# The output written by POOL's indirect DMAs instead of SP's plain ones, in a three-stage macaron block on one core

## What is computed

```
def _L0_ffn_ref(x, gate_w, gate_b, w1, b1, w2, b2, w3, b3):
    logits = einsum('bsd,de->bse', x, gate_w) + gate_b
    probs = softmax(logits, axis=1)
    vals, idx = top_k(probs, 2)
    h = relu(einsum('bsd,edo->ebso', x, w1) + b1)
    h = relu(einsum('ebso,eop->ebsp', h, w2) + b2)
    y = relu(einsum('ebso,eop->ebsp', h, w3) + b3)
    onehot = one_hot(idx, E)
    w_tok = einsum('bske,bsk->bse', onehot, vals)
    ind = onehot.max(axis=2)
    v = einsum('ebso,bse->eo', y, w_tok)
    return einsum('bse,eo->bso', ind, v)

x = x + 0.5 * _L0_ffn_ref(_layernorm(x), ...)
x = x + _L0_attn_ref(_layernorm(x), ...)
x = x + 0.5 * _L0_ffn_ref(_layernorm(x), ...)
return x
```

## Time and profile before

| | |
|---|---|
| median of 3 runs | 1159.49 us (1155.8 to 1160.2) |
| the profiled execution | 1155.8 us, of which the span of the trace is 1154.0 us |
| busy PE / DVE / POOL / ACT | 1063.4 / 886.0 / 703.5 / 670.9 us |
| output, line L404 | 8 transfers of 256 KB by SP, landing 2.5 us after issue |

### The profile page before, as it was taken

One profiled execution on the slowest core, in us unless ns is written; L12 is line 12 of the kernel. 1 busy time (PEld: TensorE's weight loads), 2 busy tenths in 40 slices (PEclk: granted clock), 3 DMA queues, 4 the chain that ended last, 5 costly groups with the idle time before them and its releaser, 6 DMA issues.

```text
span 1154.0 us, 16851 instructions
## 1 busy us (share of the span) xinstructions
PE 1063.4 (92%) x5671; PEld 609.8 (53%) x5671; DVE 886.0 (77%) x1333; ACT 670.9 (58%) x899; POOL 703.5 (61%) x367
## 2 busy tenths in 40 slices
PE   4599999659999999999999999999999976899996
PEld 1376666335645655645655655654654523666663
DVE  9989999786766866866866866866764576999996
ACT  3388888435654654654654654654654643788882
POOL 3465555527785785785685685686685861555552
PEclk8799999879999999999999999999999988899999
DMA  5165473000101001001001001001001012576672
GB/s 151 41 136 120 97 121 73 19 1 3 39 20 38 20 21 38 20 21 38 21 20 39 20 21 38 20 20 38 20 20 39 21 38 64 87 118 101 108 110 73
DMA packets 43850, 59.25 MB, mean 51 GB/s; under 512 B 9829, under 2 KB 23174, under 8 KB 43782
## 3 DMA queue, kind: packets, MB, share of 16 engines
q1 hardware_dynamic: 43782, 58.37, 24.2%
HBM read 55.20 MB, written 2.62 MB: 50 GB/s over the span
## 4 chain that ended last, share of the span: by engine, by line
PE 60%; issue 17%; POOL 16%; DVE 6%; ACT 1%; POOLq 0%; DMA 0%; SPq 0%
PE ring L737 19%; POOL R L464 13%; PE ring L690 5%; PE ring L708 5%; PE ring L710 5%; PE ring L712 5%; PE ring L714 5%; PE ring L747 4%; PE ring L723 3%; DVE xn L1054 2%; PE ring L672 2%; POOL sum_picksT L425 1%; PE ring L674 1%; PE ring L673 1%; PE ring L647 1%
## 5 line engine op out<-in xcount | busy, mean ns | idle before, releaser
L1238 DVE TENSOR_REDUCE mx<-ring 128x2 f32<-128x1024 f32 x256 | 298.6, 1225 | 88.1 <-PE ring L690 88.1
L425 POOL TENSOR_TENSOR sum_picksT<-sum_picksT,P_wb 128x1024 f32<-128x1024 f32 x128 | 323.9, 2531 | 18.6 <-POOL sum_picksT L425 0.4
L924 ACT ACTIVATE P_wb<-ring 128x1024 f32<-128x1024 f32 x256 | 262.3, 1028 | 64.8 <-PE ring L714 40.2
L464 POOL TENSOR_TENSOR R<-t,R 128x512 fp32r<-128x512 f32 x128 | 171.1, 1337 | 160.7 <-ACT R L836 160.6
L425 POOL TENSOR_TENSOR sum_picksT<-P_wb 128x1024 f32<-128x1024 f32 x64 | 153.8, 2403 | 172.7 <-ACT P_wb L924 172.7
L737 PE MATMUL ring<-P_wb,t 128*64 128x512 f32 x1024 | 226.8, 595 | 0.0
L511 PE MATMUL ring<-R,whi 128*128 128x512 f32 (+1 forms) x384 | 170.0, 443 | 18.5 <-DVE R L1033 9.6
L513 PE MATMUL ring<-R,wlo 128*128 128x512 f32 (+1 forms) x384 | 153.1, 399 | 0.0
L512 PE MATMUL ring<-R,whi 128*128 128x512 f32 (+1 forms) x384 | 152.8, 398 | 0.0
L936 ACT COPY OZ<-ring 128x512 f32<-128x512 f32 x64 | 37.0, 587 | 199.1 <-PE ring L737 156.5
L737 PEld LDWEIGHTS ring<-P_wb,t 128*64 128x64 f32 x1024 | 70.6, 137 | 132.8 <-issue 128.4
(11 more groups left out here) (136 smaller groups left out, 1350.5 us busy)
## 6 DMA issues: line engine op xcount, KB each, us to landing
P_wb<-wd SPq DMA_DIRECT2D x14, 2048.0 KB, 15.5
rzb_indp<-rzd SPq DMA_DIRECT2D x64, 256.0 KB, 3.9
P_wb<-wd SPq DMA_DIRECT2D x8, 512.0 KB, 10.4
xs<-in_L_attn_x SPq DMA_DIRECT2D x8, 256.0 KB, 3.7
zrc<-SZ SPq DMA_DIRECT2D x128, 2.0 KB, 1.7
out<-xs SPq DMA_DIRECT2D x8, 256.0 KB, 2.5
sum_picksT<-in_L_ffn_w SPq DMA_DIRECT2D x2, 512.0 KB, 5.5
MR<-mT SPq DMA_DIRECT2D x64, 4.0 KB
```

The costliest lines, as they stand in the source:

```text
L425: pool.tensor_tensor(US[:, g % 2, c, :, :], first, PU[:, TPB * c + t, :, :], ALU.add).then_inc(s_ua, 1)
L464: pool.tensor_tensor(h2l[:, e % 2, :], t2[:, e % 2, :], h2h[:, e % 2, :].bitcast(F32), ALU.subtract).then_inc(s["h2_ready"], 1)
L924: act.activation(PU[:, u, :, :], ring[slot(("scores", g, u))][:, :, :], ACT.Exp, scale=SCALE).then_inc(s_exp, 1)
L1238: dve.tensor_reduce(mx[:, :, u], ring[slot(("max", g, u))][:, :, :], AX.X, ALU.max).then_inc(s_max, 1)
```

## The change

The output is no longer sent by SP. A new tile `rows` ([128, 32] of uint32) is filled by POOL at the very start of its program with `rows[p, t] = 128 t + p`, the number of the output row that partition p of token tile t belongs to. At the end of POOL's program, behind `experts(1)`, POOL waits for the same semaphore `x_updated` batch by batch, and for every token tile issues an indirect DMA: it takes the 128 rows of 512 bytes of `xs[:, t, :]` and writes each to the row of the output (seen as 4096 rows of 128 numbers) that `rows[:, t]` names. These are 32 transfers of 64 KB where there were 8 of 256 KB. POOL then waits for all 32 (`s_out` at 512). The bytes and their places are the same.

```
         xs = sb("xs", [P, NT, D])
+        rows = sb("out_rows", [P, NT], mybir.dt.uint32)
...
+        s_rowids = sem("out_row_numbers")
...
             weights_out(1)
-            for b in range(B):
-                sp.wait_ge(F[1]["x_updated"], b + 1)
-                sp.dma_start(out[b].rearrange("(j p) d -> p j d", p=P), xs[:, TPB * b:TPB * (b + 1), :]).then_inc(s_out, 16)
-            sp.wait_ge(s_out, 16 * B)
...
         def _(pool):
+            pool.iota(rows[:, :], pattern=[[P, NT]], base=0, channel_multiplier=1).then_inc(s_rowids, 1)
             pool.memset(ident[:, :], 0.0).then_inc(s_id0, 1)
...
             experts(1)
+
+            pool.wait_ge(s_rowids, 1)
+            table = out.rearrange("b s d -> (b s) d")
+            for b in range(B):
+                pool.wait_ge(F[1]["x_updated"], b + 1)
+                for j in range(TPB):
+                    t = TPB * b + j
+                    pool.indirect_dma_start(table, bass.IndirectOffsetOnAxis(ap=rows[:, t:t + 1], axis=0), xs[:, t, :], None
+                                            ).then_inc(s_out, 16)
+            pool.wait_ge(s_out, 16 * NT)
```

## The result

| | before | changed |
|---|---|---|
| median | 1158.03 us (4 runs, 1155.8 to 1160.2) | 1192.88 us (4 runs, 1192.35 to 1196.28) |
| ratio | | 1.0307, 95% interval 1.0277 to 1.0338 |
| profiled execution, its span | 1155.8, 1154.0 us | 1196.28, 1194.5 us |
| end of DVE's first addition to the end of the span ("the ending") | 10.0 us | 45.9 us |

The account below looks back on a forecast made before the run. PE was busy 92%, but the end was bound by DVE's last addition plus one landing. Ending 32 x 1.27 + 2.5 + 0.5 = 43.6 us against 10.0, +33.6 on 1159.49: 1193.1 us, range 1168 to 1230 us.

Follow-up runs that it names:

- one-by-one kernel: The changed kernel with POOL waiting for each indirect transfer's landing before it issues the next; spacing 2.50 us, ending 83.9 us.

## What to carry to other kernels

Count the issues that an engine must make after the last result exists, multiply by the spacing of issues back to back, and compare with the pace at which the producer hands out tiles: up to that pace they are free, above it the whole queue of issues, counted from the first tile, is the length of the ending. An indirect transfer costs its issuer nearly the same for 64 and for 128 rows, so give each 128 rows rather than 64, and keep data whose place is known on plain transfers. Look behind the last wait too: an engine's closing instructions can depend on what it did all through the program.

## What was not expected of the hardware

- POOL's closing drain takes 0.08 us for each transfer that POOL issued in the program (0.394 us for 4, 5.294 us for 64), landed or not, plain or indirect.
- An indirect transfer with two semaphores to wait for has a semaphore instruction of its own ahead of it. Where that is released last, the issue starts 0.84 to 0.92 us after the release, where there is one semaphore 0.27 to 0.29 us. Where it is released early, as for seven transfers of the one-by-one kernel, nothing is lost. Why was not found.
- Behind each indirect issue POOL is idle for 0.30 us, behind a plain one not: 32 plain issues of 0.537 us follow each other 0.536 us apart. What fills these 0.30 us was not found.
